# A cross-attention whose probabilities change places with the context: 24 short matmuls per tile for two long ones, and no running sum

## The chip, the cores and the metric

The kernel runs on one core of a Trainium2 chip. The metric is the device time of one execution in microseconds (us), lower is better.

## What is computed

The reference takes latents x (16 batches of 64 rows, 256 wide) and a context (16 batches of 1601 rows, 128 wide) through three blocks: a cross-attention with 16 heads, a self-attention and a gated attention. The change touches the first:

```python
q = rmsnorm((layernorm(x) @ Wq).reshape(B, 64, 16, 128), gq)
k = rmsnorm((ctx @ Wk).reshape(B, 1601, 16, 128), gk)
v = (ctx @ Wv).reshape(B, 1601, 16, 128)
attn = softmax(einsum('bqhd,bkhd->bhqk', q, k) / sqrt(128))
x = x + einsum('bhqk,bkhd->bqhd', attn, v).reshape(B, 64, 2048) @ Wo
```

Wk is folded into the queries beforehand, and Wv and Wo are multiplied with each other later, so the big loop works on the context alone. For each batch it needs, for all 16 x 64 = 1024 pairs of head and query: the scores (context times folded query), divided by the norm of the key, their exponential, the sum of the exponentials over the 1601 context rows (the denominator), and the context summed with the exponentials as weights.

## The kernel before

A batch's context is cut into 13 tiles of 124 or 123 rows, so there are 16 x 13 = 208 tiles. All engines run through the same software pipeline (`pipeline`, `step`). A step t works on up to five tiles at once: x = t+5 is transposed and split into a high and a low part (cTh, cTl), k = t+4 gets its key projection (`key_chunk`) and the products for the norms, r = t+3 gets its inverse norm, s = t+2 gets its scores (`score_half`) and their scaling, v = t is weighed (`weigh_half`). 26 steps (two batches) are the body of a hardware loop, with the first and the last steps written out around it. The order of each engine is the order in which its `step` calls its functions; engines wait for each other by semaphores. There is no scheduler.

TensorE (PE) per tile: nine matmuls of 512 columns for the keys, into the two banks of psK in turn (L807), six of 512 columns for the scores, into the two halves of psS (L818), one transpose of the context tile into psT (L850), and the weighing (L827): two matmuls with the context tile stationary and 512 columns of probabilities moving, in plain float32. A plain float32 matmul shows as two matmul records in the trace; the other matmuls work on values rounded for one pass (high and low parts, type fp32r) and show as one. So psO gathers the sums of a batch with the context's 128 columns on the partitions and head-and-query along the row.

GpSimd (POOL) adds each tile's exponentials to a running sum `acc` (L1529; the first of a batch L1526), and small operations make the inverse norms (L1505 to L1519). Once per batch `denominators` multiplies `acc` with a matrix of ones on PE (L836, two float32 matmuls), ScalarE (ACT) and VectorE (DVE) form the inverse (L1201, L1206, L1429, L1434), ACT and DVE copy psO out (L1212, L1259) and POOL multiplies (L1497).

DVE per tile: three products of a key chunk with the doubled context (L1235), the scaling of the two halves of the scores (L1252), cTl (L1269) and a sum over the products of eight heads (L1242). ACT per tile: squares of four heads (L1013), sums of the products of four heads (L1021), the exponential (L1027), cTh (L1065) and two small functions for the norm. Once per batch, in four pieces, the context is split: a high part on ACT (L1051), a low part and the doubled context on POOL (L1443, L1450); the next batch's queries are split likewise (L1043, L1458).

SyncE (SP) loads a context batch when the batch that lies in its place has been weighed. Before the loop come the queries (to 139 us), behind it the product with Wv and Wo (`end`: `matrices` L905, `segment` L922), and then the two self-attentions, none of which the change touches in substance.

Of the kernel before, what the change touches and what calls it, by code (L numbers as in the profile page):

```python
# [51 lines left out]
def rows_of(n):  # L52

    return ROWS if n % NT < REST else FULL
# [17 lines left out]
PIECES = [slice(NT * n // 4, NT * (n + 1) // 4) for n in range(4)]  # L72


HIGH_AT, LOW_AT, TWICE_AT = (4, 6, 11, 13), (5, 7, 12, 14), (6, 11, 13, 15)
QUERY_HIGH_AT, QUERY_LOW_AT = (2, 8), (3, 9)

# [117 lines left out]
def queries(nc, T, psum, dram):  # L195
    psT, psK, psS, psO, psM = psum
    with ExitStack() as ctx:
# [82 lines left out]
        def _(pool):  # L280
# [5 lines left out]
            nc.gpsimd.memset(T.zero[:, :], 0.0).then_inc(S.consts, 1)  # L286
# [127 lines left out]
        def _(act):  # L414
# [39 lines left out]
            act.wait_ge(S.consts, 5)  # L454
# [127 lines left out]
MAIN_SEMS = ("ct cth ctl kmm ksq kprod ksum smm zz expd acc vmm nath nat c2 kadd qh ql oev_a oev_d den dlog dinv dneg dfull norm")  # L582
KEY_SEMS = "x log guess squared scaled rest root"
HEAD_SEMS = "wv wv3 wo0 wo1 wo23 wqkv wout bout vT vTh vTl woh wol wvo wvoh wvol oh ol out outTa outTd back x2 high low"
# [6 lines left out]
def cross_attention(nc, T, psum, dram):  # L591
    psT, psK, psS, psO, psM = psum
    with ExitStack() as ctx:
# [4 lines left out]
        ch_all, low_all = sb("ch", [P, NT, CD], F32R), sb("low", [P, NT, CD])  # L598
        with ExitStack() as shared:
            c2_all = shared.enter_context(nc.sbuf_tensor("c_c2", [P, NT, CD], F32))  # L600
            prob_all = shared.enter_context(nc.sbuf_tensor("c_prob", [P, PROB_SLOTS, HQ], F32))
            acc_all = shared.enter_context(nc.sbuf_tensor("c_acc", [P, 2, HQ], F32))
        turned, split, turned_low = sb("turned", [P, NT * CD], F32R), sb("split", [P, PROB_SLOTS, HQ], F32R), sb("turned_low", [P, 2, HQ], F32R)
# [5 lines left out]
        unused = sb("unused", [ROWS, 2, HB, D])  # L609
        ss = sb("ss", [ROWS, 2, 7, H])  # L610
        prob, acc = prob_all[0:ROWS, :, :], acc_all[0:ROWS, :, :]
        den = sb("den", [P, 4, BANK])
# [5 lines left out]
        ch_flat, low_flat = (x[:, :, :].rearrange("p t c -> p (t c)") for x in (ch_all, low_all))  # L618
        prod_flat = prod_all[:, :, :, :].rearrange("p a g n -> p (a g n)")
        wqkv, bout = sb("wqkv", [P, WC, 3 * DIM]), sb("bout", [P, DIM])  # L620
        wqkv_flat = wqkv[:, :, :].rearrange("p k n -> p (k n)")
        stats, mv, lx = sb("stats", [P, NPAIR, 6]), sb("mv", [P, NPAIR, 2]), sb("lx", [P, GROUPS, 5, GP])
        outT = den[:, :, :].rearrange("p a n -> p (a n)").rearrange("p (k n) -> p k n", k=WC)
        xn = acc_all[:, 1, :].rearrange("p (n k c) -> p n k c", n=GP, k=WC)
# [8 lines left out]
        def wo_of(q):  # L633

            return (low_flat[:, 0:QUAD], ch_flat[:, 0:QUAD].bitcast(F32), prod_flat[:, 0:QUAD], prod_flat[:, QUAD:2 * QUAD])[q]
# [9 lines left out]
        vTh, vTl = turned[:, 0:2 * BANK], turned_low[:, 0, :]  # L645
# [56 lines left out]
        psM_all, psT_all = psM[:, :], psT[:, :]  # L702

        def den_bank(i, batch, half):

            return psT_all if isinstance(i, int) and (i, batch, half) == (NPAIR - 1, 1, 1) else psM_all

        def steps(i, last):

            for t in range(LAG, TP if last else TP + LAG):  # L710
                yield tuple(u if not last or u < TP else None for u in (t, t + 2, t + 3, t + 4, t + 5))

        def pipeline(eng, emit, end=None, begin=None):
# [3 lines left out]
            for t in range(-5, LAG):  # L717
                emit(0, *(u if u >= 0 else None for u in (t, t + 2, t + 3, t + 4, t + 5)))
                if begin is not None and t < 0:
                    begin(t + 5)  # L720
            with eng.Fori(0, NPAIR - 1) as i:
# [11 lines left out]
        def out_half(i, batch, half):  # L733

            pair, b = i + batch // 2, batch % 2
            big = T.big[:, :].rearrange("p (n b m) -> p n b m", b=2, m=HQ)
            n = slice(pair, pair + 1) if isinstance(pair, int) else bass.ds(pair, 1)
            return big[:, n, b, half * BANK:(half + 1) * BANK].rearrange("p n m -> p (n m)")
# [24 lines left out]
        def _(sp):  # L763
# [3 lines left out]
            with sp.Fori(0, NPAIR - 1) as i:  # L767
                for b in range(2):
                    sp.wait_ge(S.vmm, done(i, NT * (b + 1) - 1, 2))
# [5 lines left out]
            sp.dma_start(wqkv[:, :, :], dram["L0_attn_W_qkv"].rearrange("(k p) n -> p k n", p=P)).then_inc(W.wqkv, 16)  # L775
# [1352 lines left out]
```

## Time and profile before

| | us |
|---|---|
| median of 3 runs | 1527.63 |
| lowest and highest | 1527.08, 1528.84 |
| the profiled execution | 1526.53 |
| its span, first to last instruction | 1524.8 |
| PE matmul busy in the span | 1438.0 (94%) |
| PE weight load busy (beside PE) | 973.3 (64%) |
| DVE busy | 1300.6 (85%) |
| ACT busy | 1156.1 (76%) |
| POOL busy | 942.6 (62%) |

Busy time of an engine is the union of its records. A matmul's record is longer than its share of the stream, since the next one starts while it still drains: the distance between the starts of two matmuls tells what one costs, not the length of the record. In the records psK, psS, psO, psM and psT are banks of PSUM; c_ before a name means a buffer of the cross-attention, and `psO<-c_prob,raw 123*128 123x512` is a matmul whose stationary operand has 123 rows and 128 columns, with 512 columns moving. Numbers at the end of a buffer's name are left out in the trace (c_c is the doubled context c2).

### The profile page before, as it was taken

How to read it: one execution, taken by the hardware profiler on the slowest of the kernel's cores; microseconds unless marked ns; L12 is line 12 of the kernel's file. 1: busy time of each engine (PE TensorE's matmuls, PEld its weight loads, DVE VectorE, ACT ScalarE, POOL GpSimd, SP SyncE). 2: the span in 40 equal slices, each digit the busy share in tenths (PEclk: the TensorE clock that was granted, in tenths of full speed). 3: DMA queues.
4: the chain of work that ended last, by engine and by line, in shares of the span. 5: the costliest groups of instructions: out<-in, count | busy, mean ns of one | idle time of the engine just before them, and what ended most of it. 6: DMA issues, size and time to landing. Idle time of an engine off the chain costs nothing. (4 is left out here: it accounts for less than half of the span.)

```text
span 1524.8 us, 29153 instructions
## 1 busy us (share of the span) xinstructions
PE 1438.0 (94%) x6176; PEld 973.3 (64%) x6176; DVE 1300.6 (85%) x2093; ACT 1156.1 (76%) x4810; POOL 942.6 (62%) x1474
## 2 busy tenths in 40 slices
PE   5996999999999999999999999999999999976886
PEld 3664666666666666666666666666666666853554
DVE  6876888998988898889888998988998988765985
ACT  5886888787888887788878787887878877534763
POOL 4001778887878887788878787878887876010000
PEclk9998999999999999999999999999999999996998
DMA  3000000000000000000000000000001011000000
GB/s 139 37 1 1 1 1 23 7 17 17 8 22 2 23 1 22 2 22 1 22 2 22 10 13 21 3 22 2 23 1 47 1 49 42 1 1 0 8 7 15
DMA packets 9818, 25.05 MB, mean 16 GB/s; under 512 B 736, under 2 KB 6016, under 8 KB 9520
## 3 DMA queue, kind: packets, MB, share of 16 engines
q1 hardware_dynamic: 9648, 23.49, 4.3%
q14 instruction: 149, 1.22, 0.3%
q8 instruction: 21, 0.34, 0.1%
HBM read 22.44 MB, written 1.05 MB: 15 GB/s over the span
## 5 line engine op out<-in xcount | busy, mean ns | idle before, releaser
L807 PE MATMUL psK<-wkh,c_cTh 128*124 128x512 f32 x832 | 509.2, 612 | 6.1 <-DVE c_prod L1235 2.8
L1235 DVE TENSOR_TENSOR c_prod<-psK,c_c 124x512 f32<-124x512 f32 x624 | 427.0, 684 | 65.6 <-PE psK L807 61.7
L1529 POOL TENSOR_TENSOR c_acc<-c_acc,c_prob 123x1024 f32<-123x1024 f32 (+1 forms) x192 | 459.1, 2391 | 2.6 <-issue 1.4
L827 PE MATMUL psO<-c_prob,raw 123*128 123x512 f32 (+1 forms) x832 | 424.9, 591 | 0.0
L1021 ACT ACTIVATE c_unused<-c_prod 124x128 f32<-124x128 f32 x832 | 247.5, 299 | 110.5 <-DVE c_prod L1235 110.5
L1252 DVE TENSOR_TENSOR c_prob<-psS,c_ss 124x512 f32<-124x512 f32 x416 | 286.9, 690 | 50.2 <-PE psS L818 34.8
L807 PE MATMUL psK<-wkl,c_cTh 128*124 128x512 f32 x832 | 328.6, 395 | 0.0
L1027 ACT ACTIVATE c_prob<-c_prob,shift 124x1024 f32<-124x1024 f32 x208 | 238.9, 1149 | 56.7 <-DVE c_prob L1252 45.4
L1242 DVE TENSOR_REDUCE c_ss<-c_prod 124x8 f32<-124x1024 f32 x208 | 253.8, 1220 | 7.2
L1013 ACT ACTIVATE c_unused<-psK 124x128 f32<-124x128 f32 x832 | 218.8, 277 | 52.9 <-PE psK L807 37.4
L807 PEld LDWEIGHTS psK<-wkh,c_cTh 128*124 128x124 f32 x832 | 154.4, 186 | 143.6 <-issue 88.7
L807 PEld LDWEIGHTS psK<-wkl,c_cTh 128*124 128x124 f32 x832 | 155.9, 187 | 107.6 <-issue 97.7
L827 PEld LDWEIGHTS psO<-c_prob,raw 123*128 123x128 f32 (+1 forms) x832 | 157.3, 189 | 38.1 <-issue 1.0
L1013 ACT ACTIVATION_READ_ACCUMULATOR c_unused<-psK 124x1 f32 x832 | 172.1, 207 | 0.0
L818 PE MATMUL psS<-c_qwh,c_cTh 128*124 128x512 f32 x416 | 165.1, 397 | 1.1 <-issue 1.1
L818 PE MATMUL psS<-c_qwh,c_cTl 128*124 128x512 f32 x416 | 163.9, 394 | 0.0
L818 PE MATMUL psS<-c_qwl,c_cTh 128*124 128x512 f32 x416 | 163.1, 392 | 0.0
L1021 ACT ACTIVATION_READ_ACCUMULATOR c_unused<-c_prod 124x1 f32 x832 | 155.4, 187 | 0.0
L1443 POOL TENSOR_TENSOR c_low<-raw,c_ch 124x384 f32<-124x384 f32 x64 | 69.4, 1084 | 109.0 <-ACT c_ch L1051 109.0
L1505 POOL TENSOR_SCALAR c_ss<-c_ss 124x16 f32<-124x16 f32 x208 | 50.4, 242 | 125.9 <-DVE c_ss L1242 108.9
L818 PEld LDWEIGHTS psS<-c_qwh,c_cTh 128*124 128x124 f32 x416 | 76.6, 184 | 21.5 <-issue 2.0
L818 PEld LDWEIGHTS psS<-c_qwl,c_cTh 128*124 128x124 f32 x416 | 76.7, 184 | 20.5 <-issue 0.7
(312 smaller groups left out, 2311.5 us busy)
## 6 DMA issues: line engine op xcount, KB each, us to landing
raw<-in_ctx SPq DMA_DIRECT2D x16, 799.5 KB
raw<-in_L_xattn_Wq SPq DMA_DIRECT2D x3, 512.0 KB, 9.7
xs<-in_x SPq DMA_DIRECT2D x1, 1024.0 KB, 5.7
big<-in_L_xattn_Wk SPq DMA_DIRECT2D x1, 1024.0 KB, 9.0
c_prod<-in_L_xattn_Wo SPq DMA_DIRECT2D x1, 1024.0 KB, 5.2
out<-s_y SPq DMA_DIRECT2D x8, 128.0 KB, 1.7
big<-in_L_ffn_W_qkv SPq DMA_DIRECT2D x1, 768.0 KB, 12.9
c_wqkv<-in_L_attn_W_qkv SPq DMA_DIRECT2D x1, 768.0 KB, 15.9
```

Source lines behind the costliest of these rows:

```text
L807: last = nc.tensor.matmul(psK[0:ROWS, c % 2, :], x[:, slot, :], w[:, cols], start=(n == 0), stop=(n == len(terms) - 1))
L818: last = nc.tensor.matmul(psS[0:ROWS, half, :], x[:, slot, :], w[:, b, cols], start=(n == 0), stop=(n == 2))
L827: nc.tensor.matmul(psO[:, half, :], raw[0:rows, b, tile, :], prob[0:rows, probs(v), half * BANK:(half + 1) * BANK], start=(tile == 0), sto ...
L1013: last = nc.scalar.activation(unused[:, c, j, :], psK[0:ROWS, c % 2, j * D:(j + 1) * D], ACT.Square, accum_out=ss[:, k % 2, 0, h:h + 1])
L1021: last = nc.scalar.activation(unused[:, 1, j, :], prod[:, k % 2, 0, j * CD:(j + 1) * CD], ACT.Copy, accum_out=ss[:, k % 2, 0, h:h + 1])
L1027: nc.scalar.activation(prob[:, probs(s), :], prob[:, probs(s), :], ACT.Exp, bias=T.shift[0:ROWS, :]).then_inc(S.expd, 1)
L1235: nc.vector.tensor_tensor(prod[:, k % 2, c - GRAM, :].rearrange("p (h c) -> p h c", c=CD), psK[0:ROWS, c % 2, :].rearrange("p (h c) -> p h ...
L1242: nc.vector.tensor_reduce(ss[:, k % 2, 0, HB * (GRAM + 1):H], prod[:, k % 2, 1:GRAMS, :].rearrange("p a (h c) -> p (a h) c", c=CD), AX.X, ...
L1252: nc.vector.tensor_tensor(prob[:, probs(s), cols].rearrange("p (h q) -> p h q", q=SQ), psS[0:ROWS, half, :].rearrange("p (h q) -> p h q", ...
L1443: nc.gpsimd.tensor_tensor(low[:, PIECES[piece], :], raw[:, batch % 2, PIECES[piece], :], ch[:, PIECES[piece], :].bitcast(F32), ALU.subtrac ...
L1505: nc.gpsimd.tensor_scalar(ss[:, r % 2, 1, :], ss[:, r % 2, 0, :], 1.0 / D, EPS, ALU.mult, ALU.add).then_inc(R.x, 1)
L1529: nc.gpsimd.tensor_tensor(acc[0:rows, batch % 2, :], acc[0:rows, batch % 2, :], prob[0:rows, probs(s), :], ALU.add).then_inc(S.acc, 1)
```

## The change

The weighing changes sides. The 1024 probabilities of a row are cut into eight blocks of 128, and each block is the stationary operand; the context tile moves. Probabilities and context are each taken as high and low parts, and three of the four products are made, so there are 8 x 3 matmuls per tile. Two columns of ones stand behind the 128 columns of the context's high part (`ch`, now 130 wide), so column 128 of each sum is the denominator. The sums of a batch stand in three banks (blocks 0 to 2, 3 to 5, 6 and 7), with head-and-query on the partitions.

With that go: `acc`, its additions, `denominators`, the inverse by logarithm and its Newton step, the copies of psO and POOL's multiplication. New are: the high part of the probabilities on ACT (a step h = t+1 between s and v), their low part on POOL, per batch on DVE three reciprocals of a few columns and three multiplications (`normalise`), on PE eight transposes that turn the result back (`turn_out`, in the second to fourth step of the next batch; `turn_last` for the last), and on ACT three copies of what was turned. ACT sums the products of two heads instead of four, DVE those of ten instead of eight. The chunks of the key projection and the halves of the scores are spread over the steps in another order, on all engines. A context batch is loaded once the batch in its place is transposed and split. The tiles of a batch are taken from the last to the first. The loads of the output weights use other buffers; the matrix W_qkv is loaded behind the third `turn`.

```diff
-            def weigh_half(i, v, half):
-                batch, b, tile, rows = v // NT, v % TP // NT, v % NT, rows_of(v)
-                if half == 0:
-                    pe.wait_ge(S.expd, done(i, v, 1))
+            def weigh(i, v, n):
...
+                if n == 0:
+                    pe.wait_ge(S.probl, done(i, v, 1))
...
                 if tile == 0:
-                    pe.wait_ge((S.oev_a, S.oev_d)[half], batch_done(i, batch - 1))
-                nc.tensor.matmul(psO[:, half, :], raw[0:rows, b, tile, :], prob[0:rows, probs(v), half * BANK:(half + 1) * BANK],
-                                 start=(tile == 0), stop=(tile == NT - 1)).then_inc(S.vmm, 1)
+                    pe.wait_ge(S.norm, batch_done(i, batch - 1, len(BLOCKS), n + 1))
+                bank = BANK_ORDER[n]
+                for m, block in enumerate(BLOCKS[bank]):
+                    cols = slice(block * P, (block + 1) * P)
+                    out = banks[bank][:, m * CW:(m + 1) * CW]
+                    if tile == 0 and m == 0:
+                        width = len(BLOCKS[bank]) * CW
+                        nc.tensor.matmul(banks[bank][:, 0:width], probh[0:rows, v % 2, cols], ch_wide[0:rows, place(v) * CW:place(v) * CW + width], start=True, stop=False)
+                    else:
+                        nc.tensor.matmul(out, probh[0:rows, v % 2, cols], ch[0:rows, place(v), :], start=False, stop=False)
+                    nc.tensor.matmul(out, probl[0:rows, probs(v), cols], ch[0:rows, place(v), :], start=False, stop=False)
+                    last = nc.tensor.matmul(out[:, 0:CD], probh[0:rows, v % 2, cols], low[0:rows, place(v), :], start=False, stop=(tile == NT - 1 and block == BLOCKS[bank][-1]))
+                last.then_inc(S.vmm, 1)
...
-            def denominators(i, batch, half):
...
+            def turn_out(i, batch, part):
+                pe.wait_ge(S.norm, batch_done(i, batch, len(BLOCKS)))
+                for m, block in enumerate(BLOCKS[part]):
+                    last = nc.tensor.transpose(psT[:, (m + 1) * P:(m + 2) * P], weighted[:, block * P:(block + 1) * P], T.ident[:, :])
+                last.then_inc(S.turned, 1)
...
+            def probabilities_high(i, h):
+                act.wait_ge(S.expd, done(i, h, 1))
+                act.wait_ge(S.vmm, done(i, h - 2, len(BLOCKS)))
+                nc.scalar.activation(probh[:, h % 2, :], prob[:, probs(h), :], ACT.Copy).then_inc(S.probh, 1)
...
+            def probabilities_low(i, h):
+                pool.wait_ge(S.probh, done(i, h, 1))
+                nc.gpsimd.tensor_tensor(probl[:, probs(h), :], prob[:, probs(h), :], probh[:, h % 2, :].bitcast(F32), ALU.subtract).then_inc(S.probl, 1)
...
-            def add(i, s):
...
+            def normalise(i, batch, n):
...
+                nc.vector.reciprocal(inverse[:, first:first + count].unsqueeze(2), sums[:, :, CD:CD + 1]).then_inc(S.inv, 1)
...
+                nc.vector.tensor_tensor(weighted[:, first * P:(first + count) * P].rearrange("p (m c) -> p m c", c=CD), sums[:, :, 0:CD],
+                                        over(inverse[:, first:first + count], CD), ALU.mult).then_inc(S.norm, 1)
```

What this makes of PE's order. One steady step before, from the transpose of tile x on (psT transpose, psK keys, psS scores, psO weighing; high parts end in h, low parts in l):

```order
L850 MATMUL psT<-ident,raw 128x124
L807 MATMUL psK<-wkh,c_cTh 124x512
L807 MATMUL psK<-wkl,c_cTh 124x512
L827 MATMUL psO<-c_prob,raw 128x512
L807 MATMUL psK<-wkh,c_cTh 124x512
L807 MATMUL psK<-wkl,c_cTh 124x512
L818 MATMUL psS<-c_qwh,c_cTh 124x512
L818 MATMUL psS<-c_qwl,c_cTh 124x512
L818 MATMUL psS<-c_qwh,c_cTl 124x512
```

The first weighing matmul of the two stands between key chunks 1 and 2; the second stands behind chunk 3.

The same place after the change (c_high and c_split are the high and low parts of the probabilities, c_ch and c_low those of the context; the right one of each pair is the stationary operand):

```order
L888 MATMUL psT<-ident,raw 128x124
L843 MATMUL psS<-c_qwh,c_cTh 124x512
L843 MATMUL psS<-c_qwl,c_cTh 124x512
L843 MATMUL psS<-c_qwh,c_cTl 124x512
L866 MATMUL psO<-c_ch,c_high 128x130
L867 MATMUL psO<-c_ch,c_split 128x130
L868 MATMUL psO<-c_low,c_high 128x128
L866 MATMUL psO<-c_ch,c_high 128x130
L867 MATMUL psO<-c_ch,c_split 128x130
L868 MATMUL psO<-c_low,c_high 128x128
```

Three such triples follow each other, then key chunk 3 (two matmuls), two triples into psM, key chunk 0 (three), three triples into psO, the other half of the next tile's scores (three), key chunks 1 and 2 of tile x (four): 15 matmuls of 512 columns as before, and 24 short ones.

One steady step of DVE after the change, from the scaling of the second half of the scores on:

```order
L1300 TENSOR_TENSOR c_prob<-psS,c_ss 124x512
L1325 TENSOR_TENSOR c_cTl<-psT,c_cTh 128x124
L1283 TENSOR_TENSOR c_prod<-psK,c_c2 124x512
L1300 TENSOR_TENSOR c_prob<-psS,c_ss 124x512
L1291 TENSOR_REDUCE c_ss<-c_prod 124x10
L1283 TENSOR_TENSOR c_prod<-psK,c_c2 124x512 x2
```

The kinds of instructions are those of before; the products of chunks 1 and 2 have moved to the end of the step, where they belong to tile x, and the sum is over ten heads.

## Rows read from the trace of the kernel before

**Rows 1.** The page: TensorE, weight loads and granted clock in 40 slices of the span.
```profile
PE   5996999999999999999999999999999999976886
PEclk9998999999999999999999999999999999996998
```
**Rows 2.** Busy time by stretch: PE, PEld, DVE, ACT, POOL, granted clock, DMA share, GB/s.
```profile
400.00:800.00 400.00, 398.49 (x1484) 265.85 (x1482) 357.78 (x540) 322.72 (x1521) 322.63 (x506) 1.00 0.03 11
```
**Rows 3.** Groups of 400 to 800 us: shapes, count, busy us, mean ns, idle before.
```profile
L850 PE MATMUL psT<-ident,raw 124*128 124x124 f32 x73 | 19.7, 270 | 0.0
L807 PE MATMUL psK<-wkh,c_cTh 128*124 128x512 f32 x293 | 180.0, 614 | 1.5 <-DVE c_prod L1235 1.4
```
**Rows 4.** Timeline of PE, one step: start us, record's length, instruction.
```profile
603.19 0.39 PE L818 MATMUL psS<-c_qwh,c_cTl 128*124 128x512 f32 x1
603.42 0.27 PE L850 MATMUL psT<-ident,raw 124*128 124x124 f32 x1
...
603.76 0.39 PE L807 MATMUL psK<-wkl,c_cTh 128*124 128x512 f32 x1
...
605.07 0.39 PE L807 MATMUL psK<-wkl,c_cTh 128*124 128x512 f32 x1
...
606.47 1.02 PE L827 MATMUL psO<-c_prob,raw 123*128 123x512 f32 x2
607.33 1.02 PE L836 MATMUL psM<-c_acc,ones 124*128 124x512 f32 x2
```
**Rows 5.** Timeline of PE in the last steps of the cross-attention.
```profile
1282.78 1.88 PE L827 MATMUL psO<-c_prob,raw 123*128 123x512 f32 x4
1284.50 0.60 PE L888 MATMUL psT<-ident,raw 128*128 128x128 f32 x4
1284.93 1.88 PE L827 MATMUL psO<-c_prob,raw 123*128 123x512 f32 x4
```
**Rows 6.** Timeline of PE in the queries: twelve matmuls of 128 columns, fp32r (first, last).
```profile
45.98 0.40 PE L408 MATMUL psO<-q_qgh,q_wkTl 128*128 128x512 f32 x1
...
46.28 0.27 PE L352 MATMUL psM<-q_wkTl,q_wkTh 128*128 128x128 f32 x1
...
47.39 0.28 PE L352 MATMUL psM<-q_wkTh,q_wkTl 128*128 128x128 f32 x1
47.51 0.45 PE L393 MATMUL psK<-q_xTh,q_wqh 128*128 128x512 f32 x1
47.80 0.39 PE L393 MATMUL psK<-q_xTh,q_wql 128*128 128x512 f32 x1
```
**Rows 7.** Timeline of PE behind the cross-attention: twelve of 256 columns (first, last).
```profile
1315.36 0.28 PE L905 MATMUL psK<-c_qwh,c_turned 128*128 128x256 f32 x1
...
1316.67 0.28 PE L905 MATMUL psK<-c_qwh,c_turned_low 128*128 128x256 f32 x1
```
**Rows 8.** Groups of the page on DVE, ACT and POOL.
```profile
L1529 POOL TENSOR_TENSOR c_acc<-c_acc,c_prob 123x1024 f32<-123x1024 f32 (+1 forms) x192 | 459.1, 2391 | 2.6 <-issue 1.4
...
L1252 DVE TENSOR_TENSOR c_prob<-psS,c_ss 124x512 f32<-124x512 f32 x416 | 286.9, 690 | 50.2 <-PE psS L818 34.8
...
L1027 ACT ACTIVATE c_prob<-c_prob,shift 124x1024 f32<-124x1024 f32 x208 | 238.9, 1149 | 56.7 <-DVE c_prob L1252 45.4
L1242 DVE TENSOR_REDUCE c_ss<-c_prod 124x8 f32<-124x1024 f32 x208 | 253.8, 1220 | 7.2
L1013 ACT ACTIVATE c_unused<-psK 124x128 f32<-124x128 f32 x832 | 218.8, 277 | 52.9 <-PE psK L807 37.4
```
**Rows 9.** One line's instructions: the query's low part on POOL, ns min/median/max.
```profile
L1458 POOL TENSOR_TENSOR c_qwl<-big,c_qwh x32: 1267/1287/1303, 146.4 to 1209.5; 128x512 fp32r<-128x512 f32 x32
```
**Rows 10.** Timeline of the loop's first tile, POOL and DVE.
```profile
141.01 1.00 POOL L1443 TENSOR_TENSOR c_low<-raw,c_ch 124x384 f32<-124x384 f32 x1 [108.28 <-ACT c_ch L1051]
142.10 1.00 POOL L1450 TENSOR_TENSOR c_c<-raw,c_low 124x384 f32<-124x384 f32 x1
143.64 0.69 DVE L1235 TENSOR_TENSOR c_prod<-psK,c_c 124x512 f32<-124x512 f32 x1 [2.79 <-PE psK L807]
```

More of the change, by code:

```diff
@@ L830, in denominators @@
-            def denominators(i, batch, half):
-                if half == 0:
-                    pe.wait_ge(S.acc, done(i, NT * (batch + 1) - 1, 1))
-                if den_bank(i, batch, half) is psM_all:
-                    pe.wait_ge(S.dneg, batch_done(i, batch, 2, half))
-                nc.tensor.matmul(den_bank(i, batch, half), T.ones[0:ROWS, :], acc[:, batch % 2, half * BANK:(half + 1) * BANK],
-                                 start=True, stop=True).then_inc(S.den, 1)
-            def step(i, v, s, r, k, x):
-                if k is not None:
-                    key_chunk(i, k, 0)
-                if s is not None:
-                    score_half(i, s, 0)
+                last.then_inc((S.s0, S.s1)[half], 1)
@@ new lines, in weigh @@
+            def weigh(i, v, n):
+                batch, tile, rows = v // NT, v % NT, rows_of(v)
+                if n == 0:
+                    pe.wait_ge(S.probl, done(i, v, 1))
+                    for piece, tiles in enumerate(PIECES):
+                        if tile == tiles.start:
+                            pe.wait_ge(S.nat, batch_done(i, batch, len(PIECES), piece + 1))
+                    if v == 0:
+                        pe.wait_ge(W.unit, BLANK // P + 2)
+                if tile == 0:
+                    pe.wait_ge(S.norm, batch_done(i, batch - 1, len(BLOCKS), n + 1))
[11 more added lines that the diff above has]
+                last.then_inc(S.vmm, 1)
@@ L875, in step, with turn_last @@
                     turn(1)
+            def turn_last():
+                pe.wait_ge(W.vTl, 2)
+                pe.wait_ge(S.norm, batch_done(LAST, 1, len(BLOCKS)))
+                for bank, half in ((psT, 0), (psM, 1)):
+                    for m in range(HB):
+                        block = half * HB + m
+                        last = nc.tensor.transpose(bank[:, m * P:(m + 1) * P], weighted[:, block * P:(block + 1) * P], T.ident[:, :])
+                    last.then_inc(W.lastT, 1)
             def turn(q):
@@ L969, in end @@
             def end(i, batch):
[L970 to L971 removed]
                 matrices(1)
+                turn_last()
                 segment(0)
@@ new lines, in step @@
+            def step(i, v, h, s, r, k, x):
+                finished = v is not None and v % NT == NT - 1
+                if s is not None:
+                    scale_scores(i, s, 1)
+                if x is not None:
+                    dve.wait_ge(S.cth, done(i, x, 1))
+                    dve.wait_ge(S.s0, done(i, x - before(CT_SLOT, x), 1))
+                    nc.vector.tensor_tensor(cTl[:, CT_SLOT[x % TP], :], psT[:, 0:ROWS], cTh[:, CT_SLOT[x % TP], :].bitcast(F32),
+                                            ALU.subtract).then_inc(S.ctl, 1)
+                if finished:
+                    normalise(i, v // NT, 0)
+                if k is not None:
+                    products(i, k, 3)
@@ L1484, in begin @@
                     context_twice_low(0, 0, 0)
-                if n in (1, 2):
-                    query_low(0, 0, n - 1)
+                if n == 1:
+                    for half in range(2):
+                        query_low(0, 0, half)
                 if n in (2, 3, 4):
```

427 lines of the change are left out of this document (204 added, 223 removed).

## The prediction

> **What bounds the kernel now.** I read the page first: TensorE is 94% busy, and in the slices of the big loop its digit is 9 throughout at a granted clock of 9 tenths or more [rows 1]. That does not yet say it is the bound, since a matmul's record includes its drain. So next the busy time by stretch: from 400 to 800 us PE is busy 398.5 of 400 us at clock 1.00, while DVE has 357.8, ACT 322.7 and POOL 322.6 [rows 2]. The groups of the same stretch show 73 transposes, one per tile, and 1.5 us of idle time ahead of the keys' matmuls [rows 3]; 400 / 73.3 gives 5.46 us per tile. Last the timeline, for what a matmul costs from start to start. From 605.07 to 606.47 stand six 512-column matmuls, 0.233 us each [rows 4]. A weighing matmul costs 0.86 us (606.47 to 607.33 [rows 4]; four records, two matmuls, in 1.72 us [rows 5]). The transpose costs 0.10: from 603.19 to 603.76 are 0.57 us, less two long ones [rows 4]. So a tile is 15 x 0.233 + 0.10 + 2 x 0.86 = 5.32, and the denominators add 2 x 0.86 per 13 tiles, 0.13: 5.45 against 5.46 found. **PE's stream is the bound, with nearly no waits in it**, and what the change does to that stream decides.
>
> **The weighing.** Two matmuls of 0.86 us go, 1.72 per tile; 24 short ones come, with 128 or 130 columns moving, a fresh 128-column stationary operand each, both fp32r. The order shows a different operand in every one of them (high, low, high), so no load can be shared. The trace has this shape exactly: twelve matmuls in the queries, also in threes into one place. Their starts are 0.111 us apart (46.28 to 47.39 is ten steps), and with the seams on both sides, from 45.98 to 47.80, they cost 1.82 less 2 x 0.233 = 1.35 us, so 0.02 more than 12 x 0.111 for a group [rows 6]. That is not the columns' time: at 0.233 per 512, 128 columns would take 0.058. Twelve matmuls with twice the columns stand 0.119 apart [rows 7]. Halving the columns saves next to nothing, so something of fixed length per matmul sets the pace, and the weight load is the thing that each has. Per tile: 24 x 0.111 + 3 groups x 0.02 = 2.73 us. **The step costs +1.01 us per tile, +210 us for 208 tiles.**
>
> The Trainium skill ("TensorE: Matmul & The Clock Gate", section "Back-to-back issue gap") says that a sustained stream of load and matmul pairs goes at about 81 ns each for 128 columns; an estimate from that page makes the weighing 1.94 us and the whole sum about 1565. The Trainium skill's same page, section "LDWEIGHTS (loading the stationary operand)", gives a load its columns divided by 1.2 per ns, 107 ns for 128; by that the sum stays as it is, and the row's 111 ns speaks for this one of the two.
>
> **The rest of PE's stream.** The denominators' 32 matmuls go: -32 x 0.86 = -27.5. Eight transposes per batch come, 128 of them. Four of 128 x 128 take 0.43, 1284.50 to 1284.93 [rows 5], so +14. The first matmul of each bank in a batch is up to 390 columns wide: 390 x 0.233 / 512 = 0.18, 0.07 above the short one, 48 times: +3.
>
> **The other engines.** None must become the bound; the new period of PE is 3.50 + 0.10 + 2.73 + (8 x 0.11 + 0.2) / 13 = 6.41 us.
> - DVE had 357.8 / 73.3 = 4.88 us per tile [rows 2]. Ten heads instead of eight are a quarter of 1.22 more, +0.3 [rows 8]. Per batch the four Newton operations and a copy go (0.69 each taken as the scaling of 512 columns, rows 8; -3.4), and 1024 columns of normalising (1.4) and three reciprocals come (at most 0.69 each): in all about 5.2.
> - ACT had 4.40 [rows 2]. The high part of the probabilities has the exponential's size, +1.15 [rows 8]; two product sums of four go, and the copies of a batch replace others. About 5.0.
> - POOL had 4.40. The addition of 2.39 goes [rows 8], the subtraction comes: the query's low part, half as wide and of the same type, takes 1.29 [rows 9], so 2.4 to 2.6. The two multiplications of the batch, of that half's size, go too. About 4.4.
> I cost these at nothing: PE's 6.41 cover them. If the cover went, DVE's 5.2 would be next.
>
> **The waits that are new.** I laid one step out on PE from its transpose: scores to 0.8, three blocks to 1.8, key chunk 3 to 2.3, two blocks to 3.0, chunk 0 to 3.7, three blocks to 4.7, scores to 5.4, chunks 1 and 2 to 6.3. Chunk 3 waits for a product that DVE made at the end of the step before, by some 0.3; ready 1.5 us early. Chunk 1 waits for cTl, ready by about 2.0 behind cTh on ACT. Chunk 2 waits for the squares of chunk 0: 4 x 0.28 [rows 8] behind 3.9, so 5.0, 0.9 us early, the tightest one. The weighing waits for POOL's low part: it starts behind ACT's high part at 2.0 and ends by 4.6, over 2 us ahead of the next step's first block; the pieces of the context, one per step at most, are passed by POOL before that and delay it by about 0.3. A new batch waits for `normalise` of the old one: the last bank is free at about 1.7 of the next step and wanted at 3.7. Queued behind these waits is all of PE, so each miss would cost its whole length. I find none: 0.
>
> **Ends.** The loop's first keys' product now stands behind four small fillings and the split of the first context piece, which the row shows on POOL from 141.0 to 143.1 with the first product at 143.64 [rows 10]. The fillings come first and the first key chunk waits longer: I take +3, between 0 and +6. The last batch loses the wait for its denominators and gains a turn; 0, within 2. The context loads may start earlier and are hidden in either case: PE has no idle time for them inside the loop.
>
> **The sum**: 210 + 3 + 14 - 27.5 + 3 = +203. The profiled execution took 1526.5, which is 1.1 below the median of the runs, so 1729.5 against it and 1730.5 against the median. I say **1730**.
>
> **Rivals.**
> 1. *A new wait inside the step.* The tightest chain is chunk 0, squares on ACT, chunk 2; ACT has the exponential and the new copy in the same queue. It decides where ACT reaches the squares more than 0.9 us late. If PE then misses 0.3 us per tile, 62 us more: 1792. For it: ACT's and DVE's work per tile grows and DVE already waits for PE in places [rows 8]. Against: all three engines get a longer period than they had, with a margin of over 1 us.
> 2. *The loads are half hidden.* Twelve matmuls are a short sample; a long stretch might go at a pace between the load's 0.111 and the columns' 0.058, say 0.085. Then the weighing is 2.04, +66 instead of +210: 1586. For it: nothing in the rows but the shortness of the sample. Against: the pace does not change over its ten steps [rows 6]. The 81 ns of the Trainium skill ("TensorE: Matmul & The Clock Gate", "Back-to-back issue gap") would be about this case.
> 3. *The other side: faster.* The loads are wholly hidden behind the matmuls, as they are for the long ones, and only columns count. The weighing is then 24 x 0.058 = 1.40 per tile, -0.32 x 208 = -67, with the rest of the sum -7: 1453, or some 20 more since DVE's 5.2 per tile would now bound it: about 1475. It decides where a short matmul costs under 0.073 us (1.72 plus 0.035 of what the batch gives back, divided by 24). The rows stand against it: halving 256 columns to 128 gave 0.008 us, not 0.06 [rows 6, 7].
> 4. *The order does not do what it says*, with fewer matmuls after building: the order shows all 24 in each steady step. No chance of its own.
>
> **How the numbers follow.** Forecast 0.82, rival 1 0.10, rival 2 0.05, rival 3 0.03. The forecast's own range: down to 0.109 per matmul and no seams, -25; up to the 0.119 of the 256-column row, +40. With the ends that is 1705 to 1770, which holds most of the 0.82; the range 1700 to 1775 takes in the mild cases of rival 1. A measurement of this kernel can tell 0.2%, 3 us, from no change. Faster 0.03, the same 0.01, slower 0.96.
>
> **What would show it.** In the new profile: PE busy nearly all of the loop, starts of L866 to L868 0.111 us apart, 6.4 us per tile between transposes L888, DVE's busy share down to about 80% of the loop, and the weight loads' share up. Wrong would be: starts 0.06 to 0.09 apart; a granted clock under 1 in the loop; or idle time of PE ahead of L832 or L866 with ACT, DVE or POOL named.

## The result and the profile after

| | before | changed |
|---|---|---|
| median, us | 1527.36 (4 runs) | 1758.03 (4 runs) |
| lowest and highest | 1526.41, 1528.84 | 1755.6, 1760.89 |
| the profiled execution | 1526.53 | 1757.07 |
| its span | 1524.8 | 1755.2 |

The changed kernel takes 1.1505 times as long (95% interval 1.1488 to 1.1521): 28 us more than the 1730 forecast, inside the range. The page first: busy time, and the 40 slices that answer to [rows 1].

```profile
PE 1655.2 (94%) x10400; PEld 1402.9 (80%) x10400; DVE 1297.7 (74%) x2110; ACT 1180.8 (67%) x4156; POOL 904.1 (52%) x1441
...
PE   6996999999999999999999999999999999995886
PEld 4664888888888888888888888888888888883554
...
PEclk9998999999998999999999999999899999996997
```

TensorE is as full as before, with 10400 matmuls; the loads' share rose from 64 to 80%, DVE's fell from 85 to 74%. Two slices of the loop have a clock digit of 8 that [rows 1] does not have there. The window that answers to [rows 2], in the same columns:

```profile
400.00:800.00 400.00, 394.99 (x2468) 347.70 (x2468) 297.29 (x455) 274.56 (x1075) 257.15 (x410) 0.97 0.03 10
```

There is the surprise: PE is busy for 3.5 us less than in [rows 2], and the granted clock averages 0.97 in place of 1.00. Away from that, the step looks as it was laid out. PE's timeline for one step (start us, length of the record, instruction; what is left out goes on in the same spacing):

```profile
705.82 0.27 PE L888 MATMUL psT<-ident,raw 124*128 124x124 f32 x1
...
706.62 0.23 PE L866 MATMUL psO<-c_ch,c_high 123*128 123x130 f32 x1
706.69 0.27 PE L867 MATMUL psO<-c_ch,c_split 123*128 123x130 f32 x1
706.80 0.27 PE L868 MATMUL psO<-c_low,c_high 123*128 123x128 f32 x1
706.91 0.28 PE L866 MATMUL psO<-c_ch,c_high 123*128 123x130 f32 x1
...
707.47 0.27 PE L868 MATMUL psO<-c_low,c_high 123*128 123x128 f32 x1
707.58 0.44 PE L832 MATMUL psK<-wkh,c_cTh 128*124 128x512 f32 x1
707.86 0.39 PE L832 MATMUL psK<-wkl,c_cTh 128*124 128x512 f32 x1
...
712.08 0.27 PE L888 MATMUL psT<-ident,raw 124*128 124x124 f32 x1
```

From 706.69 to 707.47 are seven steps of 0.111 us, and from transpose to transpose 6.26 us. Nine short matmuls cost 0.96 (706.62 to 707.58), and the long one behind them 0.28 instead of 0.23. The groups of the page say who waits for whom:

```profile
L1283 DVE TENSOR_TENSOR c_prod<-psK,c_c 124x512 f32<-124x512 f32 x624 | 411.2, 687 | 312.9 <-PE psK L832 311.1
L1561 POOL TENSOR_TENSOR c_split<-c_prob,c_high 124x1024 fp32r<-124x1024 f32 x208 | 497.1, 2390 | 91.0 <-ACT c_high L1083 91.0
L1063 ACT ACTIVATE c_unused<-psK 124x128 f32<-124x128 f32 x832 | 218.4, 277 | 344.2 <-PE psK L832 344.2
L832 PE MATMUL psK<-wkh,c_cTh 128*124 128x512 f32 x832 | 354.8, 426 | 4.0 <-DVE c_cTl L1325 2.3
...
L866 PE MATMUL psO<-c_ch,c_high 123*128 123x130 f32 (+1 forms) x1216 | 319.4, 263 | 1.0 <-POOL c_split L1561 1.0
```

DVE and ACT sit idle for over 300 us in all for PE's keys (ACT had 52.9 [rows 8]), while PE idles 4.0 and 1.0 us for them. Of PE's own idle time in the loop nearly all stands at one line, the transpose. The trace on that line:

```profile
L888 PE MATMUL psT<-ident,raw x208: 269/270/465, 140.2 to 1487.0; 124*128 124x124 f32 x104
its engine sat idle before it (us, times) until:
  issue: 31.2, 12
```

And one of them in PE's timeline, with the idle time ahead of it in brackets:

```profile
559.67 0.47 PE L888 MATMUL psT<-ident,raw 124*128 124x124 f32 x1 [2.46 <-issue]
```

Those 12 are six on the loads and six on the matmuls, at 390.37, 559.67, 733.61, 904.25, 1074.86 and 1245.75 us: one iteration of the hardware loop apart. The transpose is the first instruction of the loop body. So TensorE stands for 2.3 to 2.5 us each time that its loop jumps back, and for nothing that another engine does. What follows each jump is in the windows of 20 us around them (the columns of [rows 2]):

```profile
388.00:408.00 20.00, 17.72 (x104) 15.61 (x104) 12.37 (x20) 11.08 (x43) 12.55 (x20) 0.91 0.02 7
557.00:577.00 20.00, 17.54 (x75) 15.18 (x75) 9.24 (x14) 7.78 (x34) 9.03 (x14) 0.66 0.02 6
731.00:751.00 20.00, 17.45 (x94) 15.40 (x93) 11.39 (x18) 10.55 (x40) 10.82 (x19) 0.83 0.02 7
902.00:922.00 20.00, 17.75 (x94) 15.70 (x95) 11.36 (x18) 10.88 (x43) 11.16 (x20) 0.83 0.02 6
1072.00:1092.00 20.00, 17.73 (x93) 15.26 (x92) 11.34 (x17) 10.44 (x40) 10.84 (x19) 0.83 0.03 9
1243.00:1263.00 20.00, 17.52 (x76) 15.11 (x75) 9.22 (x14) 7.70 (x33) 9.03 (x14) 0.66 0.02 7
```

The clock goes between its two levels only, so 0.66 over 20 us are 13.6 us at the lower one (1.2 GHz), 0.83 are 6.8, 0.91 are 3.6: 51 us in all six. At half the speed that loses 26 us; PE's idle time in the six windows is 120 less 105.7, 14 us. Together 40 us. What is fetched at the jump is in the page's part on queues (packets, MB, share), of the kernel before and then of the changed one:

```profile
q8 instruction: 21, 0.34, 0.1%
```
```profile
q8 instruction: 90, 1.47, 0.4%
```

Before, no packet of this queue lies between 330 and 1205 us: the loop body stayed loaded. Now it has nine in 170 us (575 to 745), one iteration's length, and so on through the loop. The queue is TensorE's: with TensorE alone written out it has 79 packets, and with the other three engines' loops written out too it still has 79.

### The profile page after: what moved, and what is told of

The parts are those of the page before. It is cut to its first block and busy times, and to the rows that moved or that the text cites. A ratio compares the mean times of both kernels' runs of the same rounds, so it can differ in the third digit from the quotient of the medians.

```text
span 1755.2 us, 35634 instructions
## 1 busy us (share of the span) xinstructions
PE 1655.2 (94%) x10400; PEld 1402.9 (80%) x10400; DVE 1297.7 (74%) x2110; ACT 1180.8 (67%) x4156; POOL 904.1 (52%) x1441
## 5 line engine op out<-in xcount | busy, mean ns | idle before, releaser
L1561 POOL TENSOR_TENSOR c_split<-c_prob,c_high 124x1024 fp32r<-124x1024 f32 x208 | 497.1, 2390 | 91.0 <-ACT c_high L1083 91.0
L832 PE MATMUL psK<-wkh,c_cTh 128*124 128x512 f32 x832 | 354.8, 426 | 4.0 <-DVE c_cTl L1325 2.3
L868 PE MATMUL psO<-c_low,c_high 123*128 123x128 f32 (+1 forms) x1248 | 344.7, 276 | 0.0
L867 PE MATMUL psO<-c_ch,c_split 123*128 123x130 f32 (+1 forms) x1248 | 344.2, 276 | 0.0
L832 PE MATMUL psK<-wkl,c_cTh 128*124 128x512 f32 x832 | 332.4, 400 | 0.0
L866 PE MATMUL psO<-c_ch,c_high 123*128 123x130 f32 (+1 forms) x1216 | 319.4, 263 | 1.0 <-POOL c_split L1561 1.0
L1291 DVE TENSOR_REDUCE c_ss<-c_prod 124x10 f32<-124x1280 f32 x208 | 306.9, 1476 | 0.4 <-POOL c_ss L1538 0.2
L867 PEld LDWEIGHTS psO<-c_ch,c_split 123*128 123x128 f32 (+1 forms) x1248 | 241.9, 194 | 18.6
L866 PEld LDWEIGHTS psO<-c_ch,c_high 123*128 123x128 f32 (+1 forms) x1216 | 235.6, 194 | 19.7 <-POOL c_split L1561 1.2
L868 PEld LDWEIGHTS psO<-c_low,c_high 123*128 123x128 f32 (+1 forms) x1248 | 242.5, 194 | 0.0
L1083 ACT ACTIVATE c_high<-c_prob 124x1024 fp32r<-124x1024 f32 x208 | 219.0, 1053 | 0.0
L843 PE MATMUL psS<-c_qwh,c_cTh 128*124 128x512 f32 x416 | 194.3, 467 | 3.1 <-DVE c_prob L1300 3.1
L832 PEld LDWEIGHTS psK<-wkh,c_cTh 128*124 128x124 f32 x832 | 157.8, 190 | 27.9 <-DVE c_prod L1283 3.0
L832 PEld LDWEIGHTS psK<-wkl,c_cTh 128*124 128x124 f32 x832 | 157.4, 189 | 20.5
L843 PE MATMUL psS<-c_qwh,c_cTl 128*124 128x512 f32 x416 | 166.3, 400 | 0.0
L843 PE MATMUL psS<-c_qwl,c_cTh 128*124 128x512 f32 x416 | 166.2, 400 | 0.0
```

The costliest lines, as they stand in the source:

```text
L832: last = nc.tensor.matmul(psK[0:ROWS, c % 2, :], x[:, slot, :], w[:, cols], start=(n == 0), stop=(n == len(terms) - 1))
L843: last = nc.tensor.matmul(psS[0:ROWS, half, :], x[:, slot, :], w[:, b, cols], start=(n == 0), stop=(n == 2))
L866: nc.tensor.matmul(out, probh[0:rows, v % 2, cols], ch[0:rows, place(v), :], start=False, stop=False)
L867: nc.tensor.matmul(out, probl[0:rows, probs(v), cols], ch[0:rows, place(v), :], start=False, stop=False)
L868: last = nc.tensor.matmul(out[:, 0:CD], probh[0:rows, v % 2, cols], low[0:rows, place(v), :], start=False, stop=(tile == NT - 1 and block ...
L1083: nc.scalar.activation(probh[:, h % 2, :], prob[:, probs(h), :], ACT.Copy).then_inc(S.probh, 1)
```

## The experiments

Each ratio below is to runs of the kernel before that were taken beside that experiment (medians 1528.2 to 1529.7), so a difference of two medians and one of two ratios can be some us apart. "Written out" means this edit, in which TensorE's loop becomes straight code of the same instructions:

```diff
-            with eng.Fori(0, NPAIR - 1) as i:
-                for v in steps(i, False):
-                    emit(i, *v)
+            if eng is nc.tensor:
+                for i in range(NPAIR - 1):
+                    for v in steps(i, False):
+                        emit(i, *v)
+            else:
+                with eng.Fori(0, NPAIR - 1) as i:
+                    for v in steps(i, False):
+                        emit(i, *v)
```

### What the jump costs

**The changed kernel, TensorE written out.**

> The changed kernel with TensorE's loop written out: its seven iterations stand one behind another, the other engines keep their loops. Theory 1 (the loop's edge): each jump back leaves TensorE without instructions for about 2.4 us, six times, and the granted clock falls to half behind each of them; without jumps both go, 15 us of idle time and about 25 us of slower stretches: 1718 us (1710 to 1728), granted clock of the cross-attention 1.00. Theory 2 (the short matmuls themselves let the clock fall): the clock keeps falling, only the idle time goes: 1743 us (1738 to 1750). Theory 3 (neither; the idle time moves elsewhere, since another engine is what is late at the edge): 1755 to 1761 us.

1719.97 us (1718.66 to 1723.53), ratio 1.1248 (1.1228 to 1.1267): 38 us less. The window 400 to 800 of its trace:

```profile
400.00:800.00 400.00, 399.10 (x2552) 351.37 (x2551) 306.54 (x470) 284.67 (x1112) 265.28 (x427) 1.00 0.03 11
```

No idle time on issue is left on the transposes, and the clock is whole. Instruction packets still come (79), one behind the other, and cost nothing. It is thus not fetching, but fetching after a jump.

**The kernel before, TensorE written out.**

> The kernel before with TensorE's loop written out, as a control. Its trace shows no idle time of more than 0.3 us at the edge of the loop and a granted clock of 1.00. Theory 1: nothing to gain, 1527 us within 3. Theory 3 (jumps cost every kernel something that the trace hides): 1505 to 1520 us.

1528.73 us (1527.75 to 1532.1), ratio 1.0001 (0.9992 to 1.0011), with 45 packets in place of 21. A body that stays loaded costs nothing at its jump.

**The kernel before, two iterations in TensorE's body** (the seventh written out behind it). The loop then runs three times, so it jumps back twice, where seven iterations jump back six times.

> The kernel before with two iterations in TensorE's loop body and half the jumps (the seventh iteration written out behind). Theory 1a (the price of the edge comes with the length of the loop body, which no longer stays loaded): the instruction packets of 16 KB, which pause between 338 and 1221 us before, come all through the loop (over 50 instead of 21), and at the two or three jumps TensorE idles 1 to 3 us, with a fall of the clock behind: 1530 to 1550 us. Theory 1b (the price comes from how the changed kernel's step ends, not from the length): packets may come, but no idle time, 1527 us within 3.

```diff
+                with eng.Fori(0, (NPAIR - 1) // 2) as j:
+                    for i in (2 * j, 2 * j + 1):
+                        for v in steps(i, False):
+                            emit(i, *v)
```

1536.76 us (1533.04 to 1537.89), ratio 1.0046 (1.0031 to 1.006). Same work, a third of the jumps, and slower by 7 us by the ratio, 8 by the medians; 54 packets, and in the window idle time and a clock under 1, as in the changed kernel. PE stands 3.7 us at the first jump (1.9 and 1.7 in two places) and 2.2 at the second. Its window, and the second pause at the first jump in PE's timeline:

```profile
400.00:800.00 400.00, 392.74 (x1450) 261.97 (x1448) 350.17 (x526) 315.05 (x1485) 314.82 (x492) 0.99 0.03 12
```
```profile
497.49 0.58 PE L826 MATMUL psS<-c_qwh,c_cTl 128*124 128x512 f32 x1 [1.74 <-issue]
```

So the length of the body alone makes the price. From the windows one can see how long each body is. The window 400 to 800 has 2468 matmuls in 61.5 steps of the changed kernel (one per 6.51 us, 140.2 to 1487.0 in 207), 40 each, so some 1040 in the 26 steps of a body; before it was 20 each (1484 in 73.3), some 525. To these come the loads, waits and the jump, of which the trace has 1142 and 703 between two jumps. The body of before with some 1230 records stays loaded; twice that, and the changed one's 2190, do not.

The Trainium skill ("Runtime: NRT & Kernel Launch", section "Instruction fetch mechanics") has this rule: fetching is ahead of the engine as long as the code is straight, and a taken branch to something no longer loaded has to wait for a fetch. The trace agrees, with 2.3 to 2.5 us per jump. The section also gives TensorE room for 2048 instructions, by which a body of 2190 does not fit and one of 1230 does. I had not weighed it in the prediction.

**The changed kernel, two iterations in TensorE's body.**

> The changed kernel with two iterations in TensorE's loop body, the seventh written out behind it: 3 jumps back in place of 6, the same work. Theory 1 (the price is paid per jump): half of the 38 us go, 1758 less 19, 1734 to 1744 us, with issue waits of 2 to 3 us at 3 places. Rival (the price is paid per fetched instruction, since every packet is fetched again in every iteration): 1755 to 1761 us.

1735.73 us (1733.98 to 1737.72), ratio 1.1352 (1.1337 to 1.1367): 22 us less, inside the range. But the expectation counted the jumps wrongly. Three runs of the loop are two jumps back, not three, and the trace has the pause in two places (us, times, longest):

```profile
PE psT L896 <- issue: 4.9, 2, 2.6
```

So four jumps of six went, and by the theory 25 us of the 38 should go. With 22 the price per jump is 5.6 us for the four and 7.9 for the two that are left (15.8 us above the written-out form), around the 6.3 of all six. The price is paid per jump, and not per fetched packet: 83 still come.

### What the pace of the short matmuls is made of

**Half of the moving columns**, 66 and 64 in place of 130 and 128; half of each weighted sum is left out.

```diff
...
-                    nc.tensor.matmul(out, probl[0:rows, probs(v), cols], ch[0:rows, place(v), :], start=False, stop=False)
...
+                    nc.tensor.matmul(out[:, CD - 64:CW], probl[0:rows, probs(v), cols], ch[0:rows, place(v), CD - 64:CW], start=False, stop=False)
...
```

> The changed kernel with half the moving columns in the short matmuls (66 and 64 instead of 130 and 128; the first 64 columns of the weighted sums get the first matmul of a batch alone), stationary operands and count unchanged. Theory A (the weight load sets the pace): starts stay 0.111 us apart, a tile 6.2 to 6.3 us at full clock; 1758 us within 10 (a lower clock in longer stretches may add some). Theory B (the columns set it, at a rate of their own for short ones): 24 x 64 columns at 0.233 us per 512 is 0.70 us per tile, 146 us less: 1612 us. In between, 0.09 us apart: 1650 us.

1768.71 us (1764.97 to 1775.32), ratio 1.1573 (1.1544 to 1.1602). The starts stay 0.11 apart:

```profile
705.83 0.28 PE L868 MATMUL psO<-c_low,c_high 123*128 123x64 f32 x1
705.94 0.28 PE L866 MATMUL psO<-c_ch,c_high 123*128 123x66 f32 x1
706.05 0.28 PE L867 MATMUL psO<-c_ch,c_split 123*128 123x66 f32 x1
706.16 0.28 PE L868 MATMUL psO<-c_low,c_high 123*128 123x64 f32 x1
```

Half the columns bring nothing, and it is 10 us slower. By windows of 20 us around its six jumps the pauses are as long as in the changed kernel (14 us in all), but the clock is 1.00, 0.74 and four times 0.66, 65 us at the lower level instead of 51, which is 7 of the 10 us.

**Half of the stationary columns**, 64 in place of 128 in the eleven middle tiles of a batch, TensorE written out. Half of the rows' sums lack those tiles.

```diff
+                    some = P if tile in (0, NT - 1) else P // 2
...
+                    few = slice(block * P, block * P + some)
...
-                    nc.tensor.matmul(out, probl[0:rows, probs(v), cols], ch[0:rows, place(v), :], start=False, stop=False)
...
+                    nc.tensor.matmul(out, probl[0:rows, probs(v), few], ch[0:rows, place(v), :], start=False, stop=False)
...
```

> The changed kernel, TensorE's loop written out, with 64 instead of 128 stationary columns in every short matmul of a batch's second to twelfth tile (half of the weighted sums are left out); count and moving columns unchanged. Against the written-out kernel's 1720 us. Theory A (the load's length, by its stationary columns, sets the pace): starts in those tiles fall from 0.111 to about 0.06 us, where the 130 moving columns take over at 0.233 per 512; 24 x 0.05 = 1.2 us less in 176 tiles, PE's tile about 5.1, then DVE's 4.8 to 5.1 us near it: 1510 to 1540 us. Theory B (a fixed cost of every load and matmul pair, whatever its size): 0.111 stays, 1720 us within 10.

1558.97 us (1557.24 to 1561.66), ratio 1.0202 (1.0188 to 1.0217), 161 less than with whole loads:

```profile
701.05 0.22 PE L875 MATMUL psO<-c_low,c_high 123*64 123x128 f32 x1
701.11 0.22 PE L873 MATMUL psO<-c_ch,c_high 123*64 123x130 f32 x1
701.17 0.22 PE L874 MATMUL psO<-c_ch,c_split 123*64 123x130 f32 x1
701.23 0.23 PE L875 MATMUL psO<-c_low,c_high 123*64 123x128 f32 x1
```

0.06 us with the same 128 and 130 columns moving. The two runs settle it: the stationary columns set the pace, the moving ones do not. The time is 19 us above the upper end of what was expected; PE has waits again (394.59 us busy of 400 to 800), and POOL stands for 10.7 us at its jumps there.

**Two of three products**, low context times high probabilities left out, the loops kept.

```diff
-                    nc.tensor.matmul(out, probl[0:rows, probs(v), cols], ch[0:rows, place(v), :], start=False, stop=False)
-                    last = nc.tensor.matmul(out[:, 0:CD], probh[0:rows, v % 2, cols], low[0:rows, place(v), :], start=False, stop=(tile == NT - 1 and block == BLOCKS[bank][-1]))
+                    last = nc.tensor.matmul(out, probl[0:rows, probs(v), cols], ch[0:rows, place(v), :], start=False, stop=(tile == NT - 1 and block == BLOCKS[bank][-1]))
```

> The changed kernel, loops as they are, without the third product (low part of the context by the high part of the probabilities is left out): 16 short matmuls per tile. Theory A: 8 x 0.111 = 0.89 us less per tile, a tile 5.4 us at full clock, 185 us less: 1573 us if the jumps keep their price. The loop body is a sixth shorter, some 8 packets of 16 KB instead of 9 to 10; if it then stays loaded (packets pause in the loop), idle time and falls of the clock go too: 1535 us. Rival (another engine is right behind TensorE): a tile stays over 5.7 us with idle time of TensorE ahead of L832 or L866: 1620 us or more.

1565.33 us (1564.53 to 1567.02), ratio 1.0244 (1.0229 to 1.0258). Eight matmuls fewer per tile took off 193 us: 8 x 0.111 x 208 are 185. Its body has some 1780 records (2190 less 26 x 8 matmuls and as many loads), and still 79 packets come and PE still stands for 5.8 us at two jumps in the window (400 to 800 us). So what stays loaded ends somewhere between 1230 and 1780 records. That is below the 2048 of the section of the Trainium skill named above; whether a record is one instruction is not shown.

### The same kernel with bfloat16 parts

High and low parts of probabilities and context in bfloat16: the same 24 matmuls with the same columns, but the parts carry fewer bits of each value. The doubled context needs a rounding of its own on ACT and one more operation per piece on POOL, and the low part of the probabilities has two places in turn, like the high part.

```diff
-        high_all, weighted, inverse = sb("high", [P, 2, HQ], F32R), sb("weighted", [P, HQ]), sb("inverse", [P, H // 2])
+        high_all, splitb, weighted, inverse = sb("high", [P, 2, HQ], BF16), sb("splitb", [P, 2, HQ], BF16), sb("weighted", [P, HQ]), sb("inverse", [P, H // 2])
...
+                nc.scalar.activation(rounded[:, PLACES[piece], :], raw[:, b, PLACES[piece], :], ACT.Copy)
```

**TensorE written out.**

> The changed kernel, TensorE's loop written out, with the high and low parts of the probabilities and of the context in bfloat16 instead of fp32r (24 matmuls of 130 or 128 columns as before; per piece of the context one more rounding on ACT). In the trace before, a bfloat16 weight load of 128 columns is recorded with 104 ns, a float32 one with 139, an fp32r one with 190. Theory A1 (the load sets the pace and is shorter for two-byte values): starts 0.055 to 0.08 us apart, the weighing 1.4 to 1.9 us, a tile 5.1 to 5.5 us: 1485 to 1560 us, perhaps faster than the kernel before. Theory A2 (a load costs its columns, whatever the type): 0.107 to 0.111 us stay: 1720 us within 12.

1517.16 us (1514.65 to 1528.93, 12 runs), ratio 0.9941 (0.9922 to 0.9959): less than the kernel before. From 400 to 800 us PE is busy 392.69 us at clock 0.99, and the waits there (us, times, longest) name the other engines' jumps:

```profile
POOL c_ss L1549 <- issue: 11.0, 3, 4.1
DVE c_prob L1308 <- POOL c_ss L1568: 9.8, 4, 3.6
```

**All four engines kept as loops.**

> The kernel with bfloat16 parts with TensorE's loop kept as a hardware loop, so that only the type of the parts differs from the changed kernel. Theory 1 (the price of the jump back belongs to the length of the body, which the type doesn't alter): about 2.4 us of idle TensorE at each of 6 jumps, and a clock at half behind each, together as much as writing the loop out took off the changed kernel (38 us): 1545 to 1560 us. Rival (with shorter loads the queues refill while other engines are waited for, and only the idle time stays): 1525 to 1535 us.

1521.02 us (1519.94 to 1525.68), ratio 0.9953 (0.9938 to 0.9968), below both expectations. Writing out TensorE's loop takes 4 us off here, and 38 in fp32r. PE stands 18.3 us at its six jumps, but the other engines stand at theirs at about the same time, and writing out TensorE alone leaves those: from 200 to 1250 us PE is idle 18.5 us with its loop kept, 14.3 with it written out. And the clock fell less behind PE's own jumps: windows of 20 us around the six have 0.91, 0.91, three times 1.00 and 0.83, 14 us at the lower level in place of 51.

**All four engines written out.**

> The kernel with bfloat16 parts, with the loops of all four engines written out and not TensorE's alone. Theory 1 (an engine whose instruction stream has to be fetched anew at the jump back stands for 2 to 4 us there, whichever engine it is): in the kernel with bfloat16 parts GpSimd stood 4.1 us three times and VectorE 3.3 us behind it in 400 us of the record, and TensorE's granted clock fell at such places, so that 6 places of some 3 us and the clock's part go away: 1517 less 15 to 25, 1492 to 1502 us, with a granted clock of 1.00 in the window 400 to 800 and no wait on issue above 1 us there. Rival (TensorE has room for these pauses, since its buffers are filled ahead): 1514 to 1520 us.

1498.07 us (1493.09 to 1499.01), ratio 0.9791 (0.9775 to 0.9807), as expected. From 200 to 1250 us PE is idle for 1.4 us. The window 400 to 800, and PE's timeline in one step:

```profile
400.00:800.00 400.00, 400.00 (x3102) 299.76 (x3100) 372.31 (x570) 353.18 (x1376) 323.94 (x539) 1.00 0.04 14
```
```profile
701.31 0.22 PE L869 MATMUL psO<-c_lowb,c_high 123*128 123x128 bf16 x1
701.36 0.22 PE L867 MATMUL psO<-c_ch,c_high 123*128 123x130 bf16 x1
701.42 0.22 PE L868 MATMUL psO<-c_ch,c_splitb 123*128 123x130 bf16 x1
701.48 0.22 PE L869 MATMUL psO<-c_lowb,c_high 123*128 123x128 bf16 x1
```

0.057 us per matmul with all 128 stationary columns, which is what the columns moved cost at 0.233 per 512. The same load in fp32r holds the stream to 0.111. The Trainium skill ("TensorE: Matmul & The Clock Gate", section "Weight-path perf modes — Fast Weight Load (FWL) and DoubleRow") says that a fast load is on for 128 weights of a type other than FP32; the pace in these rows fits that for bfloat16, and fp32r, with the same 128, keeps the slower one. No run shows the mode itself.

**What of it is the loops' share?** The kernel before and the changed one with all four engines written out:

> The kernel before with the loops of all four engines written out. It separates what the bfloat16 parts are worth from what the written-out loops are. Theory 1 (a loop body that stays loaded costs nothing at its jump): the record of before has no wait of TensorE on issue at its jumps and 1.1 us at most on ScalarE's, which other work covers, so 1525 to 1531 us, ratio 0.998 to 1.002, and the kernel with bfloat16 parts and all loops written out (1498) beats it by 2%. Rival (every engine's jump costs something): 1505 to 1520 us.

1524.33 us (1522.51 to 1526.34), ratio 0.9972 (0.9962 to 0.9982): 4 us come of the loops alone, a little more than expected.

> The changed kernel with the loops of all four engines written out, where TensorE's alone gave 1720 us. Theory 1 (with loads at 0.111 us TensorE is 1 us a tile behind the time that the other engines take, and their 3 to 4 us at their jumps are covered or nearly so): 1712 to 1722 us, near TensorE's alone. Rival (the other engines' jumps reach TensorE as they do with bfloat16 parts, 23 us): 1695 to 1705 us.

1716.02 us (1714.11 to 1719.7), ratio 1.1223 (1.1207 to 1.1238), 4 us below TensorE's alone. Only with bfloat16 parts, where the other engines have nearly as much work per tile as PE (DVE is busy for 372 of 400 us), are their jumps worth 19 us (1517.16 to 1498.07; 23 by the ratios). Of the 32 us by which that kernel beats the one before (1529.72), 26 are left against its written-out form, 28 by the ratios.

## Why the prediction was right, and what it missed

The accounts in the profiled executions (1755.2 less 1524.8, +230.4), cut at the first and last weighing (the starts of L827; after the change those of the third product, L868): 162.2 and 1286.2 before, 167.5 and 1514.6 after. With TensorE written out the changed kernel has 167.7 and 1481.1, so it tells the stream from the jumps. No run takes the parts of the first row one by one but the short matmuls; the transposes, the denominators and the new order stand in it as summed.

| | predicted | measured |
|---|---|---|
| tiles and batches between the two weighings | +199.5 | +189.4 (1313.4 less 1124.0) |
| jumps of TensorE's loop | 0 | +33.7 (1347.1 less 1313.4) |
| start | +3 | +5.3 |
| behind the last weighing | 0 | +2.0 |
| sum | +203 | +230.4 |

- **The bound** was right: PE's stream, before and after.
- **The weighing**: "24 x 0.111 + 3 groups x 0.02 = 2.73 us". Twelve matmuls of another part of the trace gave the pace that 24 x 208 of them have. The first of each group costs 0.06 to 0.07, since its load lies behind a long matmul, and the long one after it 0.05 more. In the step shown: 0.96 + 0.62 + 0.96 and three times 0.05, 2.69 us. Narrow and half loads confirm that "the weight load is the thing that each has".
- **The period**: 6.33 without what comes per batch was found as 6.26, 6.41 with it as 6.345 (140.0 to 1453.4 us of the written-out form, 207 steps). So the new stream was put 14 us too high; the old one, 5.45 a tile where 5.43 are found (1124.0 / 207), was put 4 too high; the 10 between them are the first row's.
- **The covers** held: DVE 297 of 400 us, ACT 275, POOL 257, where DVE 5.2, ACT 5.0 and POOL 4.4 of 6.41 us would have been 324, 312 and 275: I took all of them too dear. PE waited 5 us in all for them at L832 and L866 (and 3.1 for DVE at L843), none of it between 200 and 1490 us. Rival 1 did not come.
- **Rivals 2 and 3** fell with the pace: 0.111, not 0.085 or 0.058. The 81 ns of the Trainium skill ("TensorE: Matmul & The Clock Gate", "Back-to-back issue gap") are not seen: fp32r pairs take 111 ns here, bfloat16 pairs 57. What rival 3 took for fp32r, only columns counting, is what bfloat16 does: 1498 us against its 1475.
- **What failed** is the step "The waits that are new ... I find none: 0". It looked at semaphores only. The change nearly doubles TensorE's instructions in a hardware loop (some 1230 to 2190 records), and that makes a wait without any semaphore, at 6 jumps: 14 us of idle time and, by the windows, 26 us of half clock behind it, 34 (profiled executions) to 38 (medians) by the written-out form. Before, it was zero, and no row of the trace of before could show it; the count of instructions in the body could. The text named "a granted clock under 1 in the loop" as a sign of error, and that was the sign.
- The 1730 were missed by 28 because 34 to 38 us were not counted, the stream came out 10 lower and the ends 4 higher. That the two large errors have opposite signs is luck; without it the miss would have been the whole 38.

**Open.** POOL's jump costs 3.5 us in the changed kernel and 0.2 in the one before, though its body is shorter now (382 records between jumps, 416 before). TensorE's fetching alone is not the cause: in the kernel before with TensorE written out packets come all through the loop and POOL waits on issue for no more than 0.2 us at a time, while in the changed kernel with TensorE written out it still stands for 3.5 us at each of its own, though TensorE has no jump there. The cause stays open.

## What to carry to other kernels

A change that cuts few long matmuls into many short ones has to be priced twice: by the load, which in fp32r with 128 stationary columns sets 0.111 us per matmul, with 128 columns moving or with 64, and by the instructions that it adds to a hardware loop. Count those of a body before the change and after it; where it may no longer stay loaded, write the loop out, which costs nothing here and gave back 38 us of 1758. And short matmuls want a type whose loads keep up with them: with bfloat16 parts the same idea gave 1498 us, 2% under the kernel before, where the precision allows it.

## What was not expected of the hardware

- Pauses of 2.3 to 2.5 us were followed by 3 to 14 us at half clock, 51 us for six. In the kernel with half the moving columns one of six such pauses was followed by none and the others by 10 to 14, 65 us in all. With bfloat16 parts pauses of 2.6 to 3.5 us were followed by 0 to 7, 14 us in all.
- Fetching instructions in straight code cost nothing measurable at 79 packets of 16 KB in the run, and a jump to code no longer loaded 2.2 to 3.8 us of TensorE's time.
- The type alone halves the pace of short matmuls, 0.111 us in fp32r and 0.057 in bfloat16, and so does halving the stationary columns of fp32r (0.060).
